# Seven products of half depth and half the tokens for half of the tile pairs of the first feed-forward matmul

## The reference

```python
x = L0_attn_x                                    # (16, 2048, 2048) f32
p = einsum('btc,dc->btd', layernorm(x), W) + b   # W is (4096, 2048)
gates, values = sigmoid(p[..., :2048]), tanh(p[..., 2048:])
hidden = scan(h[t] = gates[t] * h[t-1] + values[t])
x = x + layernorm(hidden)
h = einsum('bsd,hd->bsh', layernorm(x), ternarize(w_fc))    # w_fc (5120, 2048)
h = square(relu(h))
x = x + layernorm(einsum('bsh,dh->bsd', h, ternarize(w_proj)))
```

## Time and profile before

| | us |
|---|---|
| three runs, median (lowest to highest) | 3146.79 (3144.96 to 3147.18) |
| profiled execution, its time | 3145.42 |
| profiled execution, span of its slowest core | 3143.9 |
| cores, shortest to longest span | 3124.1 to 3143.9 |
| stage B in it | 1051.4 to 2160.2 |

### The profile page before, as it was taken

One profiled execution on the slowest core, in us unless ns is written; L12 is line 12 of the kernel. 1 busy time (PEld: TensorE's weight loads), 2 busy tenths in 40 slices (PEclk: granted clock), 3 DMA queues, 4 the chain that ended last, 5 costly groups with the idle time before them and its releaser, 6 DMA issues.

```text
span 3143.9 us, 47273 instructions; the slowest of 8 cores (3124.1 to 3143.9 us)
## 1 busy us (share of the span) xinstructions
PE 3032.6 (96%) x18205; PEld 1803.1 (57%) x18308; DVE 1409.2 (45%) x2022; ACT 1239.7 (39%) x1874; POOL 221.5 (7%) x342
## 2 busy tenths in 40 slices
PE   3889999999999899999999999999999999999997
PEld 2789988999999444444444444444444444444443
DVE  2344446666666310010776683001544454454454
ACT  2446665555555466666444444432111111111111
POOL 0000000000001100000000000000000000000000
PEclk8999999999999999999999999999999999999999
DMA  7968887877876995564778785325332333333332
GB/s 224 310 186 266 277 244 241 257 216 234 251 221 220 242 283 174 181 189 157 226 221 234 209 241 151 114 101 199 117 128 96 108 130 111 104 122 118 101 117 72
DMA packets 301487, 580.95 MB, mean 185 GB/s; under 512 B 148688, under 2 KB 194896, under 8 KB 283984
## 3 DMA queue, kind: packets, MB, share of 16 engines
q1 hardware_dynamic: 271280, 435.30, 47.7%
q0 software_dynamic: 29984, 142.62, 12.6%
HBM read 406.41 MB, written 137.89 MB: 173 GB/s over the span
## 4 chain that ended last, share of the span: by engine, by line
PE 91%; DMA 4%; DVE 2%; issue 1%; SPq 1%; ACT 1%; POOL 0%; DVEq 0%; ACTq 0%; POOLq 0%
PE psA L107 74%; PE psB L107 15%; PE psB L139 2%; SPq L103 1%; DMA slab<-wfc 1%; DVE st L95 1%; DMA slab<-W 1%; DMA xn1T<-xn 1%; DMA xin<-x 1%; DVE xr L115 0%; DMA xr<-W 0%; DMA xr<-x 0%; POOL rs L131 0%; ACT slab L87 0%; ACT xn L87 0%
## 5 line engine op out<-in xcount | busy, mean ns | idle before, releaser
L107 PE MATMUL psA<-xn1T,wq 128*128 128x512 bf16 x5017 | 1102.1, 379 | 17.3 <-DMA xn1T<-xn 11.9
L107 PE MATMUL psA<-xnT,wt 128*128 128x256 bf16 x8192 | 917.5, 274 | 67.6 <-DMA xnT<-xn 34.9
L107 PEld LDWEIGHTS psA<-xnT,wt 128*128 128x128 bf16 x8192 | 804.9, 98 | 166.0 <-issue 70.4
L107 PEld LDWEIGHTS psA<-xn1T,wq 128*128 128x128 fp8e4 x5120 | 501.4, 98 | 616.5 <-issue 14.6
L87 ACT ACTIVATE rbuf<-psA,am_fc 128x512 f32<-128x512 f32 x320 | 219.6, 686 | 522.0 <-PE psA L107 520.5
L107 PE MATMUL psA<-w,hs 128*128 128x512 fp8e4 x1600 | 349.9, 379 | 0.0
L107 PE MATMUL psB<-w,hs 128*128 128x512 fp8e4 x1600 | 349.9, 379 | 0.0
L95 DVE BATCH_NORM_STATS2 st<-xin 128x6 f32<-128x512 f32 x252 | 154.8, 677 | 295.8 <-DMA xin<-x_s 263.6
L135 DVE TENSOR_TENSOR_SCAN hTr<-gt,hTr,vt 128x256 f32<-128x256 f32 x221 | 165.1, 748 | 255.4 <-ACT vt L87 247.2
L107 PEld LDWEIGHTS psA<-w,hs 128*128 128x128 bf16 x1600 | 156.6, 98 | 188.7
L107 PEld LDWEIGHTS psB<-w,hs 128*128 128x128 bf16 x1600 | 156.5, 98 | 188.8
(11 more groups left out here) (59 smaller groups left out, 1753.1 us busy)
## 6 DMA issues: line engine op xcount, KB each, us to landing
slab<-wfc SPq DMA_DIRECT2D x160, 512.0 KB, 6.2
slab<-wpj SPq DMA_DIRECT2D x160, 512.0 KB, 5.5
h_s<-hst POOLq DMA_DIRECT2D x80, 512.0 KB, 4.7
pc<-h_s SPq DMA_DIRECT2D x64, 640.0 KB, 5.6
xr<-x POOLq DMA_DIRECT2D x32, 1024.0 KB, 7.6
x_s<-xr POOLq DMA_DIRECT2D x32, 1024.0 KB, 6.8
xin<-x_s SPq DMA_DIRECT2D x32, 1024.0 KB, 7.0
xb<-x_s SPq DMA_DIRECT2D x64, 512.0 KB, 4.6
```

Of the source, the lines that this page charges most:

```text
L107: return lambda e: e.matmul(*a, **k)
```

## The change

For 20 of the 40 hidden tiles (g and g + 20 for g = 0 to 9), chunks 1 to 7 compute a 2 x 2 block product by seven products instead of eight: weights W(r, c), r the upper or lower hidden tile, c the half of the depth; tokens X(r, c), r the half of the depth, c the half of the 512 tokens.

- `wx_make` and `wx_place` make, once, the sums and differences of the ternary weights (fp8, three extra pieces for each g in `wx`, two differences in place in `wq`), on DVE in chunk 0, 50 additions of 128x1024.
- `t_make(q)` makes five sums of parts of `xn1T[q % 2]` at the start of each chunk on DVE, 2048 elements a partition each. Four of them lie in the other `xn1T` buffer, that of the next chunk, and one in `tx`.
- `seven(q, g)` takes g and g + 1 together: seven products of 16 matmuls with 256 columns, each in one bank. ACT copies four of the banks' uses into `zb` (f32, seven buffers), DVE adds eight times a bank to a `zb`, and ACT then does relu and square from `zb`: 12 ACT and 8 DVE operations of 128x512 for four output tiles.
- The other 20 tiles stay `fc`, six of them ahead of the sevens and fourteen behind. Chunk 0 stays whole.
- The transposes of the next chunk may start only when the sevens are over (`st_end`), so `ROWS` is stepped three times in the sevens and 13 times in the first ten of the last fourteen tiles.
- `h_s` is stored two tiles at a time (HG = 2), so 160 stores of 256 KB with contiguous pieces of 512 B in place of 80 with pieces of 1024 B. From chunk 1 on eight banks turn round.
- `PREP2` goes at 0.82 steps a tile in chunk 0, then 0.72 a plain tile and 0.25 a product.
- In the last chunk the weight loads of stage C start behind the sevens.

```diff
...
-HG = 4
+HG = 2
...
-NST = 3
+NST = 4
...
+NS = 10
+NZ = 7
...
-        rbuf = [sb(rf, f"rbuf{i}", [P, CHF], F32) for i in range(2)]
+        zb = [sb(rf, f"zb{i}", [P, CHF], F32) for i in range(NZ)]
+        wq = sb(rf, "wq", [P, HT, KC * P], QDT)
+        xn1T1 = sb(rf, "xn1T1", [P, KC, CHF], BF16)
...
-        hst = [sb(rf, f"hst{i}", [P, TF, HG, P], BF16) for i in range(NST)]
+        tx = sb(rf, "tx", [P, KC // 2, CHF // 2], BF16)
+        wx = sb(rf, "wx", [P, NS, 3, KC * P // 2], QDT)
...
+        hst_a = [sb(rh, f"hst_a{i}", [P, TF, HG, P], BF16) for i in range(NST)]
...
+        def next_bank():
+            n = ring["at"] % ring["of"]
+            ring["at"] += 1
+            return ("AB"[n // 4], n % 4), (bankA + bankB)[n]
...
+        hst_free = [[] for _ in range(NST)]
+        h_mark = {q: [] for q in range(NF)}
+        nhst, nz = [0], [0]
+        z_free = [None] * NZ
+        fc_read, wx_mark = {}, {}
+        st_end = [None]
...
+        def h_store(q, i, ht, t):
+            m = POOL.dma(d_hs[i], op.dma_start(
+                out=h_d[q * TF:(q + 1) * TF, :, ht * P:(ht + HG) * P].rearrange("a p c -> p a c"),
+                in_=hst_of(q, i)[:, :, :, :].rearrange("p a s b -> p a (s b)")), t)
+            hst_free[i] = [m]
+            h_mark[q].append(m)
...
         def fc(q, ht):
...
+            key, bank = next_bank()
+            PE.wait(bank_free[key], wq_mark[ht // 4], *xn1T_mark[q])
             for ct in range(KC):
                 f = op.matmul(bank, wq[:, ht, ct * P:(ct + 1) * P], xn1T[q % 2][:, ct, :],
                               start=(ct == 0), stop=(ct == KC - 1))
...
             fc_read[ht] = t
...
+            z = z_next()
+            t = ACT.do(op.activation(out=zb[z][:, :], in_=bank, func=AF.Relu, scale=amc["am_fc"][:, :]),
+                       t, z_free[z])
+            bank_free[key] = t
...
+            if ht % HG == HG - 1:
+                h_store(q, i, ht - 1, t)
+        K2, T2 = KC // 2, CHF // 2
+        def wq_of(g, r, c):
+            return wq[:, g + HH * (r - 1), (c - 1) * K2 * P:c * K2 * P]
+        def wx_make(g, *marks):
+            DVE.wait(wq_mark[g // 4], wq_mark[(g + HH) // 4], *marks)
+            for n, (a, b) in enumerate((((1, 1), (2, 2)), ((1, 1), (1, 2)), ((2, 1), (2, 2)))):
+                t = DVE.do(op.tensor_tensor(out=wx[:, g, n, :], in0=wq_of(g, *a), in1=wq_of(g, *b), op=ALU.add,
+                                            saturate=False))
+            wx_mark[g] = t
+        def wx_place(g):
+            DVE.do(op.tensor_tensor(out=wq_of(g, 1, 2), in0=wq_of(g, 1, 2), in1=wq_of(g, 2, 2), op=ALU.subtract,
+                                    saturate=False), wx_mark[g], fc_read[g + HH])
+            wx_mark[g] = DVE.do(op.tensor_tensor(out=wq_of(g, 2, 1), in0=wq_of(g, 1, 1), in1=wq_of(g, 2, 1),
+                                                 op=ALU.subtract, saturate=False))
+        def w_operand(g, m, ct):
+            c = slice(ct * P, (ct + 1) * P)
+            if m in (1, 5, 2):
+                return wx[:, g, {1: 0, 5: 1, 2: 2}[m], c]
+            return wq_of(g, *{3: (1, 1), 4: (2, 2), 7: (1, 2), 6: (2, 1)}[m])[:, c]
+        def b_of(x, r, c):
+            return x[:, (r - 1) * K2:r * K2, (c - 1) * T2:c * T2]
+        t_mark = {}
+        def t_make(q):
+            x, o = xn1T[q % 2], xn1T[(q + 1) % 2]
+            at["t"] = {3: b_of(o, 1, 1), 1: b_of(o, 1, 2), 7: b_of(o, 2, 1), 4: b_of(o, 2, 2), 6: tx[:, :, :],
+                       5: b_of(x, 2, 2), 2: b_of(x, 1, 1)}
+            DVE.wait(fc_read[HT - 1], st_end[0], *xn1T_mark[q])
+            for m, a, b, o in ((3, (1, 2), (2, 2), ALU.subtract), (1, (1, 1), (2, 2), ALU.add),
+                               (7, (2, 1), (2, 2), ALU.add), (4, (2, 1), (1, 1), ALU.subtract),
+                               (6, (1, 1), (1, 2), ALU.add)):
+                t_mark[q, m] = DVE.do(op.tensor_tensor(out=at["t"][m], in0=b_of(x, *a), in1=b_of(x, *b), op=o))
+        def seven(q, g):
+            zi, zm = {}, {}
+            hs = {1: hst_next(), 2: hst_next()}
+            h_part = {1: 0, 2: 0}
+            def put(r, c, bank, t):
+                zi[r, c] = z = z_next()
+                zm[r, c] = ACT.do(op.copy(out=zb[z][:, :], in_=bank), t, z_free[z])
+                return zm[r, c]
+            def add(r, c, bank, t, o=ALU.add):
+                z = zb[zi[r, c]]
+                zm[r, c] = DVE.do(op.tensor_tensor(out=z[:, :], in0=z[:, :], in1=bank, op=o), t, zm[r, c])
+                return zm[r, c]
+            def finish(r, c):
+                z, i = zi[r, c], hs[r]
+                t = ACT.do(op.activation(out=zb[z][:, :], in_=zb[z][:, :], func=AF.Relu, scale=amc["am_fc"][:, :]),
+                           zm[r, c])
+                t = ACT.do(op.activation(
+                    out=hst_of(q, i)[:, 2 * c - 2:2 * c, :, :].rearrange("p a s b -> p s a b"),
+                    in_=zb[z][:, :].rearrange("p (s a b) -> p s a b", s=2, a=2), func=AF.Square), t, *hst_free[i])
+                z_free[z] = t
+                h_part[r] += 1
+                if h_part[r] == 2:
+                    h_store(q, i, g + HH * (r - 1), t)
+            for m in (3, 1, 5, 7, 4, 2, 6):
+                key, bank = next_bank()
+                PE.wait(bank_free[key], t_mark.get((q, m)), wx_mark[g], wx_mark[g + 1])
+                for s in range(2):
+                    for ct in range(K2):
+                        f = op.matmul(bank[:, s * T2:(s + 1) * T2], w_operand(g + s, m, ct), at["t"][m][:, ct, :],
+                                      start=(ct == 0), stop=(ct == K2 - 1))
+                        if s == 1 and ct == K2 - 1:
+                            t = PE.do(f)
+                        else:
+                            PE.quiet(f)
+                if m == 3:
+                    put(1, 2, bank, t)
+                    bank_free[key] = put(2, 2, bank, t)
+                if m == 1:
+                    DVE.wait(put(1, 1, bank, t))
+                    bank_free[key] = add(2, 2, bank, t)
+                if m == 5:
+                    add(1, 2, bank, t)
+                    bank_free[key] = add(1, 1, bank, t, ALU.subtract)
+                    finish(1, 2)
+                if m == 7:
+                    bank_free[key] = add(1, 1, bank, t)
+                if m == 4:
+                    DVE.wait(put(2, 1, bank, t))
+                    bank_free[key] = add(1, 1, bank, t)
+                    finish(1, 1)
+                if m == 2:
+                    add(2, 1, bank, t)
+                    bank_free[key] = add(2, 2, bank, t, ALU.subtract)
+                    finish(2, 1)
+                if m == 6:
+                    bank_free[key] = add(2, 2, bank, t, ALU.subtract)
+                    finish(2, 2)
+                yield
+            st_end[0] = t
...
         PREP2 = prep_pj(wt_read[NP - 1])
 
...
+        def prep_two(rate):
+            prep_steps(PREP2, rate)
+            if half[0]:
+                step(PREP2)
+        for ht in range(HT):
+            if ht < NP:
+                back_slot(NA - 1, ht)
+                if ht == NP - 1:
+                    a_end = (PE.sem, PE.n), (DVE.sem, DVE.n), (ACT.sem, ACT.n)
+            if ht >= 2 and ht % 2 == 0 and ht <= 32:
+                step(ROWS)
+            if ht % 4 == 1 and ht < 32:
+                wq_load(2 + ht // 4)
+            if ht >= 17 and ht % 2 == 1:
+                if ht < 37:
+                    wx_make((ht - 17) // 2, *a_end)
+            if ht >= HT - NS:
+                wx_place(ht - (HT - NS))
+            prep_two(0.82)
+            fc(0, ht)
+            back_late(ht)
+        q7_free[0] = q7_free[1] = [m for f in hst_free for m in f]
+        hst_free = [[free["xr"]] + f for f in hst_free]
+        ring["of"], ring["at"] = 8, 0
+        plain = list(range(NS, HH)) + list(range(HH + NS, HT))
+        for q in range(1, NF):
+            last = q == NF - 1
+            if last:
+                drain(PREP2)
+            t_make(q)
+            for ht in plain[:6]:
+                if not last:
+                    prep_two(0.72)
+                fc(q, ht)
+            for g in range(0, NS, 2):
+                if g in (2, 4, 6):
                     step(ROWS)
...
+                for n, _ in enumerate(seven(q, g)):
+                    if not last and n < 6:
+                        prep_two(0.25)
+            xn1T_free[(q + 1) % 2] = st_end[0]
+            if last:
+                pc_free += [(i, [st_end[0]]) for i in range(3)]
+                w7_load(3, st_end[0], *a_end)
+                for r, c in ((1, 1), (2, 2), (1, 2)):
+                    a_load(0, r, c)
+                for m in (1, 7, 6):
+                    w7_load(m, st_end[0])
+            for n, ht in enumerate(plain[6:]):
+                if not last:
+                    step(ROWS, {0: 1, 1: 1, 2: 1, 3: 2, 4: 1, 5: 1, 6: 2, 7: 1, 8: 1, 9: 2}.get(n, 0))
+                    prep_two(0.72)
+                elif n == 6:
```

(7 more changed lines are left out.)

137 lines of the change are left out of this document (47 added, 90 removed).

## The result

The changed kernel takes 3163.89 us (median of 7 executions, 3160.41 to 3177.52) where the kernel before takes 3146.79 beside it on the same chip: a ratio of 1.0063, 95% interval 1.0046 to 1.0081. The change is **slower, by 0.6%**. The forecast was 3120 us, faster, with a range to 3146: wrong in sign and outside its range. (In some executions one die ran at a lower clock; a ratio compares the means of the others, so it differs a little from that of the medians, and where only one execution was profiled its own time is given.)

A forecast was written before the change was run, and what follows sets the result against it. The prediction took PE to bound the kernel, busy nearly all the time in the changed stage. Its terms, -55 + 24 + 4 + 2 = -25 against 3145.4 us, gave 3120 us, with a range of 3090 to 3146.

The forecast's parts named there:

- PE, -55: Chunks 1 to 7: 560 matmuls of 256 columns replace 320 of 512, saving 7.9 us a chunk, 55 us in all.
- The rows, +24: Starts of chunks 4 to 7: the next rows' chain outlasts the 48.4 us behind the sevens, 6 us four times.
- DVE, 0: Ternary chunks: DVE's 122 us of work fits in PE's 130.3 with little left, so no loss.
- The prediction's own signs: Wrong if chunk-start gaps under 2 or over 12 us, DVE-named gaps in sevens, chunk 0 over 5, or distance not 109 ns.
- The bank additions' waits, 0: In the sevens, additions waiting on ACT's copies are hidden by eight banks, 8 x 1.75 us of PE's work.
- The clock, +4: PE behind the gaps at chunk starts: lower clock costs 1 us four times, 4 us.
- Chunk 0, +2: Chunk 0: more slabs and stores raise DMA work to 135 to 150 us; bounds 0 and 12 us, 2 taken.
- The stores of `h_s`: Halved pieces cost DMA 14.6 us more a chunk if piece count sets the price, nothing if bytes do.
- the `w_s` row: Comparison for `h_s` stores: `w_s` stores with 512 B pieces run at 176 GB/s, against 359 for `h_s`.
- slower: the last fourteen tiles drown in DMA: Last fourteen tiles: 57.7 to 62.8 us of DMA work does not fit in 48.4; 3167 us at worst, chance 0.10.
- DVE becomes the engine that is waited for: Ternary chunks: DVE's work plus waits makes 137 us a chunk, costing 23 us; 3120 to 3140 us, chance 0.12.

The follow-up runs named there:

- experiment 13: Changed kernel with DVE's two comparisons cut to 128 of 1024 columns from the ninth ternary slab on: 3114.86 us.
- experiment 4: Changed kernel with the three sums of each pair of ternary slabs left out from the third pair on: 3113.95 us.
- experiment 10: Changed kernel with row statistics ahead of the transpose, even slab rate and early first transpose, six plain tiles ahead: 3141.18 us, ratio 0.9961 to the kernel before.
- Experiment 8: Changed kernel with the ternary slabs' loads cut to 128 of 1024 columns: 3154.40 us in the profiled execution.
- experiment 11: Changed kernel with statistics ahead, even slab rate, early first transpose and four plain tiles ahead of the sevens: 3127.63 us, ratio 0.9921 to the kernel before.
- experiment 14: As experiment 11, with `nm` of row 1 directly behind its statistics, two products ahead of the first transpose: 3124.89 us, ratio 0.9921.

## Why the prediction was wrong, step by step

- **PE, -55**: right. 64 matmuls of 512 columns take 13.97 us as a row, 16 of 256 take 1.91 with fp8 weights too, and the chunks without gaps last 130 us.
- **The rows, +24**: the term that was furthest off; it measured 44.5. The place and the chunks were right, and the chain is real. I had 50.0 to 58.8 us for the chain and took 54.4; measured from the sevens' end it was 60.0, 59.1, 63.6 and 55.4, that is 48.4 and the gap. With DVE relieved from chunk 4 on (experiment 13) the last three were 54.1, 56.3 and 49.4, and in experiment 4 the first three 50.7, 54.9 and 54.1. So the chain by itself was sized well, and what was missing is that its statistics stand in DVE's order behind the sevens' additions: I gave the first link no row work at all, taking the second row as ready when the first transpose lands.
- **DVE, 0**: wrong, and the root of the miss. "122 us of 130.3: it fits with little left" was right in its sum (119 measured) and wrong in what it concludes. I had seen that DVE also waits, and gave that a chance of 0.12 and a chunk of 137 us; but busy time near the whole chunk does not have to exceed it to cost. DVE runs in order and its waits for ACT's copies, for slabs and rows add to the 119; behind chunk 4's sevens its last addition ended 11 us after the last product, and the second row's statistics began 13 us after it. By experiments 4 and 13 that cost some 20 to 30 us in the chain, and 10.9 inside the sevens. The prediction's own signs name it: a gap over 12 us (15.15), and gaps inside the sevens with DVE named.
- **The bank additions' waits, 0**: wrong by that 10.9; eight banks do not hide a DVE that is late by more than them.
- **The clock, +4**: 10.2, and 1.3 inside the sevens. I had scaled from a gap of 11.94 us that lost 1.9 us; gaps of 7 to 15 us lost 1.7 to 2.9.
- **Chunk 0, +2**: 0 in the profiled execution at a DMA share of 1.01. In others it was not free: experiment 10's profiled core lost 6.6 us in four gaps that ACT ended, after ACT itself had waited for slabs of the |w| sums, once for 8.03 us. The bounds of 0 and 12 held.
- **The stores of `h_s`**: between the ends. In the last chunk, from 2050 to 2125 us, twelve stores of 256 KB (960 packets, 3.15 MB) take 13.7% of 75 us, 0.86 us each or 306 GB/s, where pieces of 1024 B ran at 359: 2.5 us more of DMA time a chunk, not 14.6. The rule of the Trainium skill (DMA: Bandwidth & Descriptors, Specifications), line rate from 512 B on, is much nearer here than the `w_s` row, though the rate was 15% under that of 1024 B.
- **The rivals**: "slower: the last fourteen tiles drown in DMA" priced the outcome well (gaps near 13 us as the point where it tips) and named the wrong cause. Experiment 8 took some 30% of the DMA load away, and 37.6 of the 44.5 us of gaps and four fifths of the whole loss stayed. "DVE becomes the engine that is waited for" was the right cause; I priced it as taking the place of the rows' loss, and it comes on top of it: of the 55.4 us of gaps at the starts and in the sevens, 15 to 25 are left with DVE relieved, and 31 to 41 go.

What stays open: how much of the remaining 17 us of experiment 11 (gaps of 5.35, 2.34 and 9.26) a second `xn` or `xin` would give, which wasn't tried; and how the chain's and DVE's parts divide exactly: experiments 4 and 13 relieve DVE by different cuts and give 14.6 and 24.8 us.

## What to carry to other kernels

When a change gives an in-order engine more work, do not ask only whether its busy time fits. Ask what else stands in its queue behind the new work, and who waits for that: here a row's statistics, and with them out of the way a 0.15 us instruction, stood behind late additions and held a serial chain on which every chunk hung. Moving the small instruction alone gained next to nothing (experiment 14), since the next engine's queue was late as well. Where two buffers are merged into one, write out the chain that this makes, with each link's queue positions, and start it as early as its own half of the buffer is free; spreading the other work evenly, taking the statistics ahead, starting the chain early and giving it two more tiles of cover together turned a loss of 0.6% into a gain of 0.8% (experiment 11).
